# Writing a gate's bias into PSUM from ScalarE, with gate and difference in separate banks

## The reference

```python
a = tanh(x @ WA.T)                       # 16 states
b = x @ WB.T
g = sigmoid(x @ Wg.T + bg)               # the gate, 256 wide
dx = x @ WD.T + bD
h[t] = a[t] * h[t-1] + b[t]              # scan over 4096 tokens
y = (h @ WC.T) * g + dx * (1.0 - g)
x = layernorm(x + y)
...                                      # second layer: 1/8 of the tokens, attention, feed forward
```

## Time and profile before

| | us |
|---|---|
| median of three runs (481.13 to 481.71) | 481.47 |
| span of the profiled execution, first to last instruction | 479.4 |
| first stage, from the first products to the last L1471 | about 9 to 172 |
| PE busy, whole span | 443.7 (93%) |
| DVE busy | 396.5 (83%) |
| ACT busy | 287.3 (60%) |
| POOL busy | 182.1 (38%) |

### The profile page before, as it was taken

The page is one execution under the profiler, slowest core; times in us unless marked ns, Lnnn a source line. Parts: engine busy times, 40 slices in busy tenths (PEclk is TensorE's granted clock), DMA queues, the critical chain, the costliest instruction groups (busy, mean ns, idle before and its releaser), DMA issues.

```text
span 479.4 us, 10265 instructions
## 1 busy us (share of the span) xinstructions
PE 443.7 (93%) x3525; PEld 328.7 (69%) x3525; DVE 396.5 (83%) x1227; ACT 287.3 (60%) x617; POOL 182.1 (38%) x231
## 2 busy tenths in 40 slices
PE   8798999999999987999997999998998999999893
PEld 5687888777777742476774666676796666666592
DVE  4778898788998799868789999997966999995673
ACT  4436555565546527024768999985435999995640
POOL 8356667775677742076045000002001500000374
PEclk9899999999999999998999999999999999999998
DMA  8713342234321211046872000000000000000011
GB/s 246 253 45 91 120 142 91 88 94 135 124 89 46 79 53 45 1 131 217 332 213 76 1 3 2 1 3 1 1 1 0 3 1 2 3 2 1 0 40 50
DMA packets 29370, 33.89 MB, mean 71 GB/s; under 512 B 5860, under 2 KB 24968, under 8 KB 29320
## 3 DMA queue, kind: packets, MB, share of 16 engines
q1 hardware_dynamic: 23088, 24.78, 16.0%
q0 software_dynamic: 3520, 8.40, 5.7%
q10 hardware_dynamic: 2712, 0.06, 0.3%
HBM read 19.59 MB, written 13.63 MB: 69 GB/s over the span
## 4 chain that ended last, share of the span: by engine, by line
PE 50%; DVE 6%; POOL 5%; ACT 5%; issue 4%; POOLq 0%; DVEq 0%; ACTq 0%
PE ps L1011 12%; PE ps L1028 8%; PE ps L995 6%; PE ps L1080 3%; PE ps L1115 3%; PE ps L928 3%; PE ps L698 3%; PE ps L960 2%; PE ps L832 2%; POOL arena L519 2%; PE ps L885 1%; PE ps L1086 1%; ACT arena L1350 1%; PE ps L933 1%; PE ps L1106 1%
## 5 line engine op out<-in xcount | busy, mean ns | idle before, releaser
L1350 ACT ACTIVATE arena<-arena,nmax 128x511 f32<-128x511 f32 x128 | 91.6, 719 | 3.2 <-DVE nmax L1827 3.0
L1827 DVE CUSTOM_DVE_ANT_0 arena<-ps,nmask 128x511 f32<-128x511 f32 x128 | 84.8, 683 | 0.6 <-issue 0.6
L1011 PE MATMUL ps<-ident,arena 128*128 128x128 f32 x512 | 78.7, 276 | 4.1 <-ACT big L422 2.3
L1011 PEld LDWEIGHTS ps<-ident,arena 128*128 128x128 f32 x512 | 58.7, 140 | 25.9 <-ACT arena L1350 15.7
L731 PE MATMUL ps<-wgd_hi,x_hi 128*128 128x512 f32 x128 | 51.6, 403 | 0.0
L733 PE MATMUL ps<-wgd_hi,x_lo 128*128 128x512 f32 x128 | 50.5, 395 | 0.0
L732 PE MATMUL ps<-wgd_lo,x_hi 128*128 128x512 f32 x128 | 50.4, 393 | 0.0
L995 PE MATMUL ps<-arena 96*128 96x512 bf16 x128 | 48.4, 384 | 0.8 <-DVE x_sel L1892 0.5
L422 DVE COPY big<-ps 128x512 f32<-128x512 f32 x64 | 44.0, 688 | 5.4 <-PE ps L1011 4.1
L519 POOL TENSOR_TENSOR arena<-arena 128x512 f32<-128x512 f32 x30 | 38.8, 1293 | 9.6 <-DVE arena L1471 7.9
L422 ACT COPY big<-ps 128x512 f32<-128x512 f32 x64 | 37.0, 578 | 8.0 <-PE ps L1028 6.2
(11 more groups left out here) (267 smaller groups left out, 1033.1 us busy)
## 6 DMA issues: line engine op xcount, KB each, us to landing
arena<-in_L_attn_x SPq DMA_DIRECT2D x16, 512.0 KB, 4.6
out<-ob_sb SPq DMA_DIRECT2D x16, 512.0 KB, 3.2
w_sb<-in_L_ffn_w SPq DMA_DIRECT2D x2, 1024.0 KB, 10.3
mt_scratch<-nmask SPq DMA_DIRECT2D x8, 256.0 KB, 5.8
mt_scratch<-big SPq DMA_DIRECT2D x8, 256.0 KB
big<-in_L_attn_Wg SPq DMA_DIRECT2D x1, 256.0 KB, 4.2
big<-in_L_attn_WD SPq DMA_DIRECT2D x1, 256.0 KB, 5.2
wqk<-in_L_ffn_wq SPq DMA_DIRECT2D x1, 256.0 KB, 7.8
```

The costliest lines, as they stand in the source:

```text
L1011: mm = pe.transpose(ps[:, 2 + u % 2, k * P:(k + 1) * P], pr[u % 4][:, k * P:(k + 1) * P], ident[:, :])
L1350: act.activation(pr[u % 4][:, 0:K - 1], sm[u % 4][:, 0:K - 1], ACT.Exp, bias=nmax[:, c, h:h + 1], scale=-1.0, accum_out=rsum[:, c, h:h + 1 ...
L1827: dve.tensor_tensor_reduce(sm[u % 4][:, 0:K - 1], ps[:, S_BANKS[b][u % AHEAD], 0:K - 1], nmask[b][:, c, 0:K - 1], 1.0, 3.4e38, ALU.add, AL ...
```

## The change

- The gate of a half (two tiles of 256 columns) now fills one bank (3 for q = 0, 5 for q = 1), the difference the next one (4, 6). Every gate input product of 512 columns becomes two of 256 with the same stationary operand.
- From round 1 on the gate has no product with the state: its bias is already in the bank when the first gate product adds to it. ACT writes it there, with a copy of `bg_row` (bg on all 128 partitions), right after the sigmoid that read the bank, for the group after this one: 15 rounds of two halves. The copy waits for the sigmoid (`g_ready`) and signals `g_seeded`; PE's `gate_inputs` waits for that beside `u_ready`.
- Round 0 still brings bg by a product with the state, now of 256 columns per tile.
- The sigmoid waits for `g_done`, which the last gate input product signals, no longer for `gd_done`; DVE's product with the difference now waits for `gd_done` too.
- One more DMA, ahead of the second tile of x on SP's queue, loads `bg_row` (128x256).
- Two pairs of semaphores of the second layer are merged to one each.

```diff
+            sp.dma_start(bg_row[:, :, :], bg.rearrange(...).broadcast_to((P, 1, D))).then_inc(router_loaded, 16)
             for u in range(1, XBUF):
...
             def gate_inputs(G, q):
                 if G > 0:
+                    pe.wait_ge(g_seeded, 2 * (G - 1) + q + 1)
                     pe.wait_ge(u_ready, 2 * (G - 1) + q + 1)
...
-                        o = ps[:, 3 + 2 * q + t, :]
-                        pe.matmul(o, hi, wgd_hi[:, c, :], start=(c == 0), stop=False)
-                        pe.matmul(o, hi, wgd_lo[:, c, :], start=False, stop=False)
-                        pe.matmul(o, lo, wgd_hi[:, c, :], start=False, stop=False)
+                        pe.matmul(o[0], hi, wgd_hi[:, c, 0:D], start=(new and G == 0), ...)
+                        pe.matmul(o[1], hi, wgd_hi[:, c, D:2 * D], start=new, ...)
+                        pe.matmul(o[0], hi, wgd_lo[:, c, 0:D], start=False, ...)
+                        pe.matmul(o[1], hi, wgd_lo[:, c, D:2 * D], start=False, ...)
+                        mm = pe.matmul(o[0], lo, wgd_hi[:, c, 0:D], start=False, stop=(c == KD - 1), ...)
+                        pe.matmul(o[1], lo, wgd_hi[:, c, D:2 * D], start=False, ...)
+                if G > 0:
+                    mm.then_inc(g_done, 1)
...
-                    mm = pe.matmul(ps[:, 3 + 2 * q + t, :], h_parts[j][:, tt * P:(tt + 1) * P], wc_d[:, :], ...)
+                    mm = pe.matmul(ps[:, 4 + 2 * q, t * D:(t + 1) * D], h_parts[j][:, tt * P:(tt + 1) * P], wc_d[:, D:2 * D], ...)
...
             def gate(G, q):
-                act.wait_ge(gd_done, 2 * G + q + 1)
+                bank = ps[:, 3 + 2 * q, :].rearrange("p (t d) -> p t d", t=2)
+                act.wait_ge(g_done, 2 * G + q + 1)
...
+                act.activation(g_sb[q][:, :, :], bank, ACT.Sigmoid).then_inc(g_ready, 1)
+                if G + 1 < NGB:
+                    if G == 0 and q == 0:
+                        act.wait_ge(router_loaded, 48)
+                    act.wait_ge(g_ready, 2 * G + q + 1)
+                    act.copy(bank, bg_row[:, :, :].broadcast_to((P, 2, D))).then_inc(g_seeded, 1)
```

More of the change, by code:

```diff
@@ L136, in build @@
         rb_col = sb("rb_col", [P, 1])
+        bg_row = sb("bg_row", [P, 1, D])
         minus_half = sb("minus_half", [P, NT])
@@ L271, in build @@
         router_loaded = sem("router_loaded")
+        g_seeded = sem("g_seeded")
         gain_ready = sem("gain_ready")
@@ L290, in build @@
         parts_ready = sems("parts_ready")
-        kept_ready = sems("kept_ready")
+        kept_ready = sem("kept_ready")
         m_rows_in = sems("m_rows_in")
@@ L314, in build @@
         angle_ready = sems("angle_ready")
-        sin_ready = sems("sin_ready")
+        sin_ready = sem("sin_ready")
         rope_ready = sems("rope_ready")
@@ L357, in build @@
         h_lo_ready = sem("h_lo_ready")
+        g_done = sem("g_done")
         gd_done = sem("gd_done")
@@ L727, in gate_inputs @@
                     tt = 2 * q + t
+                    o = [ps[:, 3 + 2 * q + n, t * D:(t + 1) * D] for n in range(2)]
                     for c in range(KD):
                         hi, lo = (x[G % XS][:, c, tt * P:(tt + 1) * P] for x in (x_hi, x_lo))
-                        o = ps[:, 3 + 2 * q + t, :]
-                        pe.matmul(o, hi, wgd_hi[:, c, :], start=(c == 0), stop=False)
-                        pe.matmul(o, hi, wgd_lo[:, c, :], start=False, stop=False)
-                        pe.matmul(o, lo, wgd_hi[:, c, :], start=False, stop=False)
+                        new = t == 0 and c == 0
+                        pe.matmul(o[0], hi, wgd_hi[:, c, 0:D], start=(new and G == 0), stop=False, skip_group_check=True)
+                        pe.matmul(o[1], hi, wgd_hi[:, c, D:2 * D], start=new, stop=False, skip_group_check=True)
+                        pe.matmul(o[0], hi, wgd_lo[:, c, 0:D], start=False, stop=False, skip_group_check=True)
+                        pe.matmul(o[1], hi, wgd_lo[:, c, D:2 * D], start=False, stop=False, skip_group_check=True)
+                        mm = pe.matmul(o[0], lo, wgd_hi[:, c, 0:D], start=False, stop=(c == KD - 1), skip_group_check=True)
+                        pe.matmul(o[1], lo, wgd_hi[:, c, D:2 * D], start=False, stop=False, skip_group_check=True)
+                if G > 0:
+                    mm.then_inc(g_done, 1)
             def state_products(G, q):
@@ L740, in state_products @@
                 pe.wait_ge(h_lo_ready, G + 1)
+                if G == 0:
+                    for t in range(2):
+                        tt = 2 * q + t
+                        mm = pe.matmul(ps[:, 3 + 2 * q, t * D:(t + 1) * D], h_parts[j][:, tt * P:(tt + 1) * P], wc_d[:, 0:D],
+                                       start=False, stop=True, skip_group_check=True)
+                    mm.then_inc(g_done, 1)
                 for t in range(2):
                     tt = 2 * q + t
-                    mm = pe.matmul(ps[:, 3 + 2 * q + t, :], h_parts[j][:, tt * P:(tt + 1) * P], wc_d[:, :],
-                                   start=False, stop=True)
+                    mm = pe.matmul(ps[:, 4 + 2 * q, t * D:(t + 1) * D], h_parts[j][:, tt * P:(tt + 1) * P], wc_d[:, D:2 * D],
+                                   start=False, stop=True, skip_group_check=True)
                 mm.then_inc(gd_done, 1)
@@ L1315, in sines @@
                 act.activation(trig[b][:, 4, :, :], trig[b][:, 3, :, :], ACT.Sin)
-                act.activation(trig[b][:, 5, :, :], trig[b][:, 3, :, :], ACT.Sin, scale=0.5).then_inc(sin_ready[b], 1)
+                act.activation(trig[b][:, 5, :, :], trig[b][:, 3, :, :], ACT.Sin, scale=0.5).then_inc(sin_ready, 1)
             def copy_mask_rows(b, tiles):
@@ L1468, in products @@
                 dve.wait_ge(g_ready, 2 * G + q + 1)
+                dve.wait_ge(gd_done, 2 * G + q + 1)
                 if G > 0:
                     dve.wait_ge(s_ready, 2 * (G - 1) + q + 1)
-                dve.scalar_tensor_tensor(u_sb[q][:, :, :], g_sb[q][:, :, :], 1.0, ps[:, 3 + 2 * q:5 + 2 * q, D:2 * D],
+                dve.scalar_tensor_tensor(u_sb[q][:, :, :], g_sb[q][:, :, :], 1.0,
+                                         ps[:, 4 + 2 * q, :].rearrange("p (t d) -> p t d", t=2),
                                          ALU.subtract, ALU.mult).then_inc(u_ready, 1)
@@ L1879, in residual @@
             def residual(b):
-                dve.wait_ge(kept_ready[b], C)
+                dve.wait_ge(kept_ready, (b + 1) * C)
                 for c in range(C):
```

9 lines of the change are left out of this document (4 added, 5 removed).

## The result

The changed kernel takes **491.6 us** (median of four runs, 490.99 to 492.29). The kernel before took 481.59 beside it. The ratio is 1.0201, with a 95% interval of 1.0175 to 1.0226. The change is slower, as forecast, but by about 10 us and not by 6.9; the time lies 0.6 us above the top of the predicted range. The profiled execution took 491.05 us with a span of 488.9, against a span of 479.4 before: 9.5 us more.

The account below looks back on a forecast made before the run. The bound was taken to be the scan-to-scan ring over ACT and DVE, not PE. 10 x 0.67 + 0.2 = 6.9 us on 481.47 gave 488.4 us, range 486 to 491.

Parts of the forecast that it names:

- The ring and its two legs: First stage, scan to scan: ACT's leg 5.01 plus DVE's leg 4.43, 9.44 us; the copy adds 0.67 per round.
- The round with POOL's extra work: Round near 88 us where DVE waits 1.59 us for POOL's total; claimed to absorb the 0.67 and not grow.
- the round with the integer instructions: Round at 137.45, four small integer instructions beside POOL's total; between 0 and 0.67 us added, 0.2 taken.
- An ACT copy into PSUM: Half 1's bias copy between sigmoid and normalise on ACT; 0.49 becomes 0.63 + 0.53, 0.67 us more per round.
- The bound from below (0.49): Copy's slot on ACT taken as long as the same-sized sigmoid's, giving 0.63 us per round, 6.3 in all.
- the row of the same kind (0.53): Second layer's copy waiting for a gelu, next instruction 0.53 us after it; used as the copy's slot.
- PE's saving, counted at nothing: Gate and state products: 0.30 us less PE time per round, 4.5 in all, counted nothing since PE is outside the ring.
- The load, counted at nothing: Broadcast of 128x256 on SP ahead of x's second tile; nothing, with 1.0 us as the other end.
- Rival 3: PE's clock falls from about 1 us idle per round: 0.42 x 11 = 4.6 us on top, 493.0; chance 0.05.

Follow-up runs that it names:

- an idle copy alone: Kernel before plus an unread 128x512 SBUF-to-SBUF copy per round on ACT, waiting for the sigmoid of half 1: 490.63 us, ratio 1.0183.
- the positions on SP: Four position loads issued by SP instead of ACT, in both kernels: changed kernel 488.33 us, kernel before 480.86 us.
- the order in which PE was nearly the bound: ACT's copy of turned x of half 0 ahead of normalise: 479.74 us on the kernel before; 481.79 on the changed kernel, bias load last.
- The kernel with PE kept busy: Changed kernel plus nine idle 256-column products (24 in round 2) ahead of half 1's transposes in rounds 2 to 13: 491.42 us, ratio 1.0177.
- the later copy: Changed kernel with half 1's bias copy issued on ACT behind the copy of turned x of half 0: 484.62 us, 483.78 when run once more.
- the same with products of zero: Changed kernel with half 1's bias copy behind the copy of turned x, plus two zero-weight 256-column products per half: 484.35 us, ratio 1.0042.
- the load last: Changed kernel with the load of bg_row moved behind the two router loads on SP's queue: 491.15 us, ratio 1.0177.

## Why the prediction was too low

**The ring and its two legs** held. 0.63 and 0.53 were forecast for the copy, 0.63 and 0.52 measured; idle time 1.1 against 1.08; rounds 10.1 against 10.11. Taking the copy out of the ring gave 9.44 back, an idle copy alone gave 10.11. Ten rounds were to grow, and ten did. The round with POOL's extra work did not (0.01); of the 0.2 us taken for the round with the integer instructions, 0.10 came. With the positions on SP the whole pair of stages differs by 6.8 us, and the runs by 7.5.

**An ACT copy into PSUM.** The bound from below (0.49) was not reached; the row of the same kind (0.53) was right to 0.01. The PSUM copy lasts 0.59 us, the SBUF copy of the same size in the experiment 0.62, and their slots are 0.52 and 0.53. The Trainium skill, "ScalarE: Activation LUTs", section "Step-by-step: what each stage is for", has the PSUM write as the faster one: the trace agrees in sign, by 0.03 us in the duration and 0.01 in the slot, which is the last digit printed.

**PE's saving, counted at nothing,** brought no time even in the order in which PE was nearly the bound: 481.79 with the change and 479.74 without. It was not nothing, though: it made PE's idle time longer. In a clean round PE waits 0.69 us with the idle copy, which leaves PE its work, and 1.08 to 1.16 with the change.

**The load, counted at nothing,** was right as far as its place goes (491.15 against 491.35).

**The step that failed: half the loss beyond the ring was put into a rival as all or nothing.** Rival 3 had the clock fall in every round, at 0.42 us each, with a chance of 0.05, and the forecast had it fall in none. It fell in two rounds and cost 0.75 and 0.60 us. The argument against it was one pair of rows, an idle time of 1.06 us at 38 to 40 with the clock at 1.00. That row was true, and in the changed kernel gaps of 1.08 do no harm either. But the same part of the prediction said that PE would wait about a microsecond more in each round, and the trace of before had longer gaps than the usual one: in the third round PE already waited 1.32 us ahead of 40.26. The two rounds, in the trace of before:

```profile
40.26 0.63 PE L707 MATMUL ps<-ident,arena 128*128 128x128 f32 x4 [1.32 <-DVE x_lo L1446]
...
98.59 0.63 PE L707 MATMUL ps<-ident,arena 128*128 128x128 f32 x4 [0.86 <-DVE x_lo L1446]
```

The 1.06 us of the earlier trace rows are a part of the first of these gaps, cut off by the window's end. It should have been asked for every round what its own gap becomes (3.17 and 1.77 were the two that fell), and the outcome "in one or two rounds" should have had a price of 1 to 2 us and a place in the range. The Trainium skill, "TensorE: Matmul & The Clock Gate", section "A second HAM failure mode: psum-queue depth-cycling", told of short idle times that make the clock swing; here most rounds with such idle times kept 1.00, and two did not.

**A term that was missing.** Nothing in the sum was about ACT's four DMA issues in the third round, since the change doesn't touch them. They took 0.50 us longer, and in the same round the copy stands behind them: 1.32 + 0.67 + 0.50 gives a gap of about 2.5 us, and it was 3.17. The other 0.7 is PE's missing work. Take away from that gap the duration of the first pos_last and, where a copy is in the ring, 0.67. In the traces in which normalise still stands ahead of the copy of turned x, 0.61 to 0.72 us are left in the six in which PE has the gate's state products or idle ones in their place, 1.24 to 1.41 in the five without. (The kernel with PE kept busy is left out, as its gap is filled.) The direct pair is the later copy, whose issue took 1.31 us, and the same with products of zero, whose issue took 1.84:

```profile
40.65 1.05 PE L711 MATMUL ps<-ident,arena 128*128 128x128 f32 x4 [2.72 <-DVE x_lo L1474]
```

```profile
40.25 0.63 PE L712 MATMUL ps<-ident,arena 128*128 128x128 f32 x4 [2.49 <-DVE x_lo L1481]
```

That the longer issue on ACT goes with the longer code of 256-column products was seen in 14 of 14 traces; that the instruction packet is its cause was argued, not tried, and SP's long issues without a packet speak against it as the only one.

**The range** ended at 491, though its own parts give 481.47 + 8.4 + 0.5 + 1.0 = 491.4. It had half a microsecond for scatter, which is far too little. The first scan alone started between 11.78 and 12.85 us over all these profiles, in kernels with and without the load, and the kernel before itself ranged from 479.57 to 485.47 over the four groups of runs. Behind that scan the first round lasts 11.18 to 11.52 us in the thirteen profiles in which the clock falls at 18 to 24 us, and 9.86 to 10.08 in the five in which it does not.

## What to carry to other kernels

Find the ring that closes on itself in one round, and price an added instruction by its place in it: the same copy cost 0.67 us a round in the ring and left the round at 9.44 us when it stood 2.3 us further down the same list, and a whole normalise moved out of it made the kernel faster. Then ask of each single round, not of the usual one, how long the next engine's idle time becomes, because one long gap can cost the clock of the round that follows. Compare the DMA issues between the traces too: one of them grew here though no line of the change touches it.

## What was not expected of the hardware

- **The clock after equal gaps.** In one execution PE's clock fell behind a gap of 1.77 us (104.33) and not behind one of 1.79 (157.83); with the load last it was the other way round, 1.76 kept it and 1.78 lost it. At the end of the stage PE waits 1.51 us and then issues six products of 512 columns. Timeline of the kernel before, of the changed kernel, and of the one with PE kept busy:

```profile
171.90 1.46 PE L698 MATMUL ps<-ones_b 128*128 128x512 bf16 x6 [1.51 <-DVE arena L1466]
```

```profile
181.11 1.46 PE L702 MATMUL ps<-ones_b 128*128 128x512 bf16 x6 [1.51 <-DVE arena L1489]
```

```profile
179.86 2.72 PE L702 MATMUL ps<-ones_b 128*128 128x512 bf16 x6 [1.51 <-DVE arena L1493]
```

The same gap and the same six products, 1.46 us in two kernels and 2.72 in the third. PE had been kept busier in the third, but they are also slow in two kernels without idle products: 1.79 us with the load last, 1.96 with the later copy run once more. The length of the gap alone does not settle it, and what does was not found.

- **ACT's DMA issue and code.** The same issue of 0.5 KB took ACT 0.60 us in three traces and 0.97 to 1.84 in eleven, and the eleven are those with a packet of instruction loading just ahead of it. On SP such an issue took 1.13 to 1.41 us in four traces without one.
